# A graph layer with linear attention on one core: the work before the gathers put in another order, the gate kept turned, the gathers without a bounds operand

## The reference

```python
def _L0_gnn_ref(x, W, bias, rows, cols):
    n = x.shape[0]
    h = x @ W.T + bias
    deg = jax.ops.segment_sum(jnp.ones(rows.shape, x.dtype), rows, num_segments=n)
    norm = jax.lax.rsqrt(1.0 + deg)[:, None]
    h = norm * h
    agg = jax.ops.segment_sum(h[cols], rows, num_segments=n)
    h = agg + h
    return norm * h
...
    qkv = (x @ Wqkv).reshape(b, n, 3, h, d)
    q, k, v = (qkv[:, :, 0], qkv[:, :, 1], qkv[:, :, 2])
    k = jax.nn.softmax(k, axis=1)
    context = jnp.einsum('bnhd,bnhv->bhdv', k, v)
    out = jnp.einsum('bnhd,bhdv->bnhv', q, context).reshape(b, n, c)
    ...
    hgate = jax.nn.gelu(xn @ Wg1 + bg1, approximate=False)
    gate = jax.nn.sigmoid(hgate @ Wg2 + bg2)
    return out * gate @ Wproj + bproj
...
xn = _layernorm(x, axis=-1)
x = x + _L0_gnn_ref(xn, ..., src, dst) + _L0_mix_ref(xn[None], ...)[0]
x = x + _L0_ffn_ref(_layernorm(x, axis=-1)[None], ...)[0]
```

## Time and profile before

| | us |
|---|---|
| three runs: lowest, median, highest | 1666.53, 1668.29, 1668.53 |
| the profiled execution | 1666.09 |
| its span in the trace | 1664.4 |
| first gather issued | 473.96 |
| last gather issued | 1584.64 |
| mean granted clock of TensorE, as a share of 2.4 GHz | 0.901 |

### The profile page before, as it was taken

The page is one execution under the profiler, slowest core; times in us unless marked ns, Lnnn a source line. Parts: engine busy times, 40 slices in busy tenths (PEclk is TensorE's granted clock), DMA queues, the critical chain, the costliest instruction groups (busy, mean ns, idle before and its releaser), DMA issues.

```text
span 1664.4 us, 32504 instructions
## 1 busy us (share of the span) xinstructions
PE 1219.0 (73%) x7498; PEld 1007.9 (61%) x7499; DVE 964.7 (58%) x3571; ACT 401.8 (24%) x1361; POOL 993.5 (60%) x1055
## 2 busy tenths in 40 slices
PE   1327888869997876877877887778787877877643
PEld 1326677648875665766666666666666656666432
DVE  7799999999814542544444543444444434444347
ACT  4603656643431110111111111111111101111000
POOL 0002656640047777777777777777777777777700
PEclk9657989979998998999999998999999989999876
DMA  9100111110035556555556566655555565655624
GB/s 237 32 1 15 50 38 46 51 32 0 0 94 164 165 165 157 166 165 164 165 164 165 166 165 160 163 166 163 164 166 165 163 165 164 166 163 162 145 31 155
DMA packets 92721, 209.10 MB, mean 126 GB/s; under 512 B 29009, under 2 KB 49736, under 8 KB 92068
## 3 DMA queue, kind: packets, MB, share of 16 engines
q0 software_dynamic: 53760, 165.20, 36.4%
q1 hardware_dynamic: 24098, 25.72, 5.7%
q10 hardware_dynamic: 14834, 17.88, 3.8%
HBM read 192.31 MB, written 16.00 MB: 125 GB/s over the span
## 4 chain that ended last, share of the span: by engine, by line
POOL 30%; DVE 26%; issue 21%; PE 15%; DMA 6%; DVEq 1%; POOLq 0%; SPq 0%; ACT 0%
POOL gath L350 30%; PE bank L735 5%; DMA gath<-table,idx_stage 4%; DVE big_t L881 4%; DVE keyB L960 3%; DVE keyA L960 3%; PE bank L682 3%; PE bank L685 3%; DVE keyB L959 2%; DVE keyA L959 2%; DVE gath L879 1%; DVE kmax L952 1%; PE bank L691 1%; PE bank L578 1%; DVE big_g L1250 1%
## 5 line engine op out<-in xcount | busy, mean ns | idle before, releaser
L350 POOL DMA_INDIRECT gath<-table,idx_stage x840 | 853.6, 1016 | 370.0 <-issue 361.1
L735 PE MATMUL bank<-gath,onehot 128*125 x1680 | 353.9, 359 | 247.3 <-SPq L275 171.4
L735 PEld LDWEIGHTS bank<-gath,onehot 128*125 x1680 | 235.6, 144 | 359.4 <-issue 333.6
L1096 DVE TENSOR_SCALAR onehot<-iota_b,row_of 128x125 bf16 x840 | 170.9, 290 | 139.1 <-issue 137.6
L1107 DVE SCALAR_TENSOR_TENSOR h_res<-big_g,bank 125x256 f32<-125x256 f32 x50 | 21.1, 422 | 397.4 <-PE bank L754 397.4
L530 ACT ACTIVATE vv<-bank 128x250 f32<-128x250 f32 x50 | 19.0, 379 | 803.1 <-PE bank L775 803.1
L783 PEld LDWEIGHTS bank<-vv,w_sb 128*128 128x128 f32 x1600 | 189.6, 195 | 6.4 <-ACT vv L530 1.6
L783 PE MATMUL bank<-vv,w_sb 128*128 128x125 f32 x1600 | 189.6, 278 | 0.9 <-ACT vv L530 0.9
L793 PE MATMUL bank<-w_sb,keyB 128*125 128x256 f32 x800 | 180.9, 379 | 0.0
L793 PEld LDWEIGHTS bank<-w_sb,keyB 128*125 128x125 f32 x800 | 146.1, 188 | 19.8
L536 ACT ACTIVATE keyB<-bank,b_sb 128x125 f32<-128x125 f32 x400 | 112.9, 366 | 159.8 <-PE bank L783 149.9
(11 more groups left out here) (246 smaller groups left out, 1843.9 us busy)
## 6 DMA issues: line engine op xcount, KB each, us to landing
gath<-table,idx_stage POOLq DMA_INDIRECT x840, 3.2
table<-parts SPq DMA_DIRECT2D x50, 187.5 KB
parts<-table ACTq DMA_DIRECT2D x50, 187.5 KB
h_s<-in_x ACTq DMA_DIRECT2D x50, 125.0 KB
big_g<-in_x SPq DMA_DIRECT2D x5, 1120.0 KB
out<-big_g SPq DMA_DIRECT2D x10, 560.0 KB
w_sb<-in_L_ffn_w SPq DMA_DIRECT2D x2, 1024.0 KB
gath<-in_L_mix_Wqkv ACTq DMA_DIRECT2D x1, 768.0 KB
```

The source lines that it names most:

```text
L350: g.indirect_dma_start(out=gath[:, j, :], out_offset=None, in_=table[:, :], in_offset=bass.IndirectOffsetOnAxis(ap=idx_stage[:, j:j + 1], ...
L735: last = t.matmul(bank[0][0:P, 0:hi - lo], onehot_g[:, hot_slots, u * 128:u * 128 + P].rearrange("p a r -> p (a r)"), gath_g[:, slots, u * ...
L1096: last = nc.vector.tensor_scalar(onehot_g[:, slots, u * 128:u * 128 + P].rearrange("p a r -> p (a r)"), iota_b[:, 0:P], row_of[:, bass.ds( ...
```

## The change

1. **Before the sort.** The gate's constant and the sign step come ahead of histogram 1. Four, five and seven early sort stages (`LEADS`) stand between the histograms and behind them, ten of them before; the statistics stand behind histogram 1.
2. **Pass zero.** What needs no degree runs for all 50 windows from histogram 1 on, written out without loops: scaling, turning, storing, hidden row, keys of two windows in one product of 250 columns, gate. TensorE's last two histograms stand ahead of its windows 6 and 14. The first 16 windows of `xnT` lie in the tiles of w1 and w2 while `big_t` is in use; SP moves them and then loads w1 and w2.
3. **peek** is one instruction for two windows, 25 in all and one more at the end, and `KMAX_AT` falls from 374 to 297 quarters.
4. **One later pass** behind `kmr`: keys, values and context of window m, then the table rows of windows 2m + 2 and 2m + 3. The sorted keys are turned ahead of window 40. The copies of `xnT` into `xT` are gone, the products read `big_t`.
5. **The gate is kept turned** (128 x 250) and so is the attention's result: two transposes (L761) and ScalarE's copies (L519, L524) go from every window.
6. **The gathers** have no bounds operand.

```diff
-SORTED_BY = 19
-PEEK = 7
-LAST_PEEK = PEEK * NW
-KMAX_AT = LAST_PEEK + 24
+NB_KT = 2
+PEEK_FROM, PEEK, PEEK_LEAD = 7, 17, 12
+KMAX_AT = PEEK * (NPAIR - 1 - PEEK_FROM) + 8
+HELD = 16
+HIST_AT = (6, 14)
+KEYS_AT = 40
+LEADS = (4, 9, 16)
...
+            sp.wait_ge(s["hist"], NHIST + 1)
+            sp.wait_ge(s["xstore"], HELD)
+            for n in range(2):
+                sp.dma_start(big_t[:, n * 8:(n + 1) * 8, 0:2 * P],
+                             held[n][:, 0:8 * 2 * P].rearrange("p (w c) -> p w c", w=8)).then_inc(s["moved"], 16)
+            sp.wait_ge(s["moved"], 32)
+            sp.wait_ge(s["kT"], HELD // 2)
+            sp.dma_start(w1_sb[:, :, :], w1.rearrange("(c p) n -> p c n", p=128)).then_inc(s["wload"], 16)
+            sp.dma_start(w2_sb[:, :, :], w2.rearrange("(c p) n -> p c n", p=128)).then_inc(s["wload"], 16)
...
                     g.tensor_tensor(hgb[:, j, :], hg[:, j, :], bg1_bc[:, :], ALU.add).then_inc(s["hgb"], 1)
 
+            with g.Fori(0, NPAIR) as i:
+                for j in range(2):
+                    w = i * 2 + j
                     g.wait_ge(s["hev"], w + 3)
...
-            last_row = g.to_reg(NODES - 1)
...
-                                in_offset=bass.IndirectOffsetOnAxis(ap=idx_stage[:, j:j + 1], axis=0),
-                                bounds_check=last_row, oob_is_err=True).then_inc(s_slot[j], 16)
+                                in_offset=bass.IndirectOffsetOnAxis(ap=idx_stage[:, j:j + 1],
+                                                                    axis=0)).then_inc(s_slot[j], 16)
...
+            for m in range(NW):
+                if m + 1 < NW:
+                    stored(m + 1)
+                hidden_out(m)
+                if m:
+                    gate_turned(m - 1)
+                if m + 2 < NW:
+                    scaled(m + 2)
+                activated(m)
+                if m:
+                    gate_out(m - 1)
...
+            def h_out(m):
+                j = m % 2
+                a.wait_ge(s["main"], m + 1)
+
+                a.wait_ge(s["split"], m + 1)
+
+                a.wait_ge(s["tabfree"], m + 1)
+                a.activation(h_s[:, j, :], bank[j][0:P, 0:C], ACT.Identity, scale=norm[:, m:m + 1])
+                a.activation(parts[:, j, 0, :], bank[j][0:P, 0:C], ACT.Identity,
+                             scale=norm[:, m:m + 1]).then_inc(s["hev"], 1)
...
+            a.wait_ge(s["normd"], 1)
+            h_out(0)
...
+            h_out(1)
+            for m in range(NW):
+                exponents(m)
+                for n in (2 * m + 2, 2 * m + 3):
+                    if n < NW:
+                        h_out(n)
...
+            turn(0)
+            for m in range(NW):
+                if m in HIST_AT:
+                    histogram(2 + HIST_AT.index(m))
+                if m == HIST_AT[1]:
+                    t.matmul(bank[3][:, 0:NW], ident_b[:, :], zeros_b[:, 0:NW], start=False, stop=True,
+                             skip_group_check=True).then_inc(s["hist"], 1)
+                if m == HIST_AT[1] + 2:
+                    t.wait_ge(s["nwt"], 1)
+                    t.matmul(bank[3][:, 64:64 + NW], ones[0:P, 0:128], deg[:, :], start=True, stop=True).then_inc(s["cntp"], 1)
+                if m + 1 < NW:
+                    turn(m + 1)
+                hidden(m)
+                if m % 2:
+                    keys(m // 2)
+                if m:
+                    turn_gate(m - 1)
+                    gate(m - 1)
...
+            t.wait_ge(s["rowsh"], 1)
+            main(0)
+            main(1)
+            t.wait_ge(s["kmaxd"], NPAIR + 1)
...
+            t.wait_ge(s["kmr"], 1)
+            for m in range(NW):
+                if m == KEYS_AT:
+                    t.wait_ge(s["sortd"], 1)
+                    for b in range(COLS // 128):
+                        last = t.transpose(bank[2 + b // 4][:, (b % 4) * 128:(b % 4 + 1) * 128],
+                                           sorted_keys[:, b * 128:(b + 1) * 128], ident[:, :])
+                    last.then_inc(s["keyp"], 1)
+                keys_values(m)
+                if m:
+                    contexts(m - 1)
+                for n in (2 * m + 2, 2 * m + 3):
+                    if n < NW:
+                        main(n)
...
             def attention(m):
 
-                t.wait_ge(s["staged"], m + 1)
                 t.wait_ge(s["og"], m + 1)
-                for c in range(2):
-                    last = t.matmul(bank[1][0:P, 0:C], xT[:, 0, c, :], Wqc[:, c, :], start=c == 0, stop=c == 1)
+                for half in range(2):
+                    for c in range(2):
+                        last = t.matmul(bank[1][:, half * P:(half + 1) * P], Wqc[:, c, half * 128:(half + 1) * 128],
+                                        xnT[:, bass.ds(m, 1), c, :].rearrange("p a n -> p (a n)"), start=c == 0, stop=c == 1)
                 last.then_inc(s["op"], 1)
 
-            def turn_gated(m):
+            def project(m):
...
+            def lead(lo, hi):
+                for k, e in early[lo:hi]:
+                    local_stage(k, e, 0, EARLY, open_keys=False)
+
+            histogram(1)
+            lead(0, LEADS[0])
+            v.wait_ge(s["bna"], NW)
+            step(nc.vector.tensor_scalar(var[:, :], var[:, :], 1.0 / C, None, ALU.mult))
+            step(nc.vector.tensor_scalar(nwt[:, 0, :], var[:, :], EPS, None, ALU.add))
+            inverse_sqrt(rstd[:, :], nwt[:, 0, :], nwt[:, 1, :])
+            step(nc.vector.tensor_tensor(nmr[:, :], mean_n[:, :], rstd[:, :], ALU.mult))
+            step(nc.vector.tensor_tensor(nwt[:, 0, :], var[:, :], rstd[:, :], ALU.mult))
+            step(nc.vector.tensor_tensor(nwt[:, 0, :], nwt[:, 0, :], rstd[:, :], ALU.mult))
+            step(nc.vector.tensor_scalar(nwt[:, 0, :], nwt[:, 0, :], EPS, None, ALU.add))
+            inverse_sqrt(r2[:, :], nwt[:, 0, :], nwt[:, 1, :])
+            v.sem_inc(s["stats"], 1)
+            histogram(2)
+            for _ in range(2):
+                peek()
+            split_row(rows_h, "wmain", 16 * 9)
+            v.sem_inc(s["rowsh"], 1)
+            lead(LEADS[0], LEADS[1])
+            peek()
+            histogram(3, between=peek)
+            for _ in range(2):
+                peek()
+            lead(LEADS[1], LEADS[2])
...
-                if n < NW and stages[0] >= PEEK * (n + 1):
-                    v.wait_ge(s["kT"], n + 3)
-                    step(nc.vector.tensor_reduce(kmax2[:, :], bank[4 + 3 * (n % 2)][:, 0:2 * P].rearrange("p (h n) -> p h n", h=2),
-                                                 AX.X, ALU.max))
-                    nc.vector.tensor_tensor(kmax[:, :], kmax[:, :], kmax2[:, :], ALU.max).then_inc(s["kmaxd"], 1)
-                    v.wait_ge(s["kmaxd"], n + 3)
-                    peeks[0] += 1
+                v.wait_ge(s["kT"], n + 1)
+                nc.vector.tensor_reduce(kpart[:, n, :], bank[KT_BANK[n % NB_KT]][:, 0:4 * P].rearrange("p (h n) -> p h n", h=2),
+                                        AX.X, ALU.max).then_inc(s["kmaxd"], 1)
+                peeks[0] += 1
...
+                    if peeks[0] < NPAIR and stages[0] >= PEEK * (peeks[0] - PEEK_FROM) - PEEK_LEAD:
+                        peek()
+                        if peeks[0] == NPAIR:
+                            v.wait_ge(s["kmaxd"], NPAIR)
+                            nc.vector.tensor_reduce(kmax[:, :], kpart[:, :, :].rearrange("p i h -> p h i"), AX.X,
+                                                    ALU.max).then_inc(s["kmaxd"], 1)
...```

TensorE, around the wait for `kmr` (L682 is keys and values, L671 the turned maximum). Before, up to the loop over pairs of windows:

```order
L641 MATMUL bank<-ident,hact 64x125 [waits s_hact,s_ghT]
L646 MATMUL bank<-Wg_b,hgT 125x256 [waits s_gate,s_ghT]
L671 MATMUL bank<-ident,kmax 1x128 [waits s_gate,s_kmaxd]
L671 MATMUL bank<-ident,kmax 1x128
L675 MATMUL bank<-zeros_b,ident 128x129 x2
L682 MATMUL bank<-gath,xT 125x256 [waits s_ekv,s_stage,s_kmr]
L682 MATMUL bank<-gath,xT 125x256
L683 MATMUL bank<-rows_b,ones_b 125x256
L685 MATMUL bank<-gath,xT 125x256 x2
```

383 lines of the change are left out of this document (145 added, 238 removed).

## The result

| | before | after |
|---|---|---|
| median of the runs, us | 1667.7 | 1690.3 |
| the profiled execution | 1666.1 | 1692.7 |
| first gather issued | 473.96 | 553.21 |
| last gather issued | 1584.64 | 1611.24 |
| from there to the end of the span | 79.8 | 79.7 |

The ratio is 1.0133 (95% interval 1.0111 to 1.0155): slower by 22.6 us. The forecast was 1705, its range 1600 to 1722. But the 26.6 us between the two profiled executions are two differences, neither of which the forecast had: the first gather comes **79 us later** (it had 37), and the stretch of gathers is **52.7 us shorter** (it had 0). The tail is what it was.

A forecast was written before the change was run, and what follows sets the result against it. POOL's own pace in the 840 gathers was taken to bound two thirds of the span. The median 1668.3 plus 37 us for a later first gather, all else 0, gave 1705 us; own range 1688 to 1722, with rivals 1600 to 1722.

The forecast's parts named there:

- the front as forecast: Part before the gathers: first gather at 511 us where it was 474, a cost of 37 us.
- The gathers' price: Gathers without their bounds operand: gain taken as 0 of the 1.01 us each, the rest kept for the range.
- Rival A: Gathers: the bound was a compare per index on POOL; at 0.1 us a gather 1621 us; chance 0.38.
- Pass zero at 3.0 us a window: TensorE's windows beside the histograms: 3.0 us each, without the table row's 1.3; the sort goes on at 161 us.
- Rival C: Pass zero keeps 4.2 us a window, TensorE and ScalarE waiting in turn; sort restarts at 173, 1722 us; chance 0.05.
- Sort up to kmr: VectorE's sort of 297 quarter-stages, with transposes and reductions: 140 us, so kmr at 301 us.
- The rows: Table rows in the later pass: 7.1 us a pair beside the sort, 6.6 behind; POOL's last row kmr + 171.
- That the end of keys and values "adds nothing": Later pass: keys and values end at kmr + 227, before the 17th gather needs its slot, adding nothing.
- the sentence that the time is the first gather plus a fixed rest: Whole span: the time is the start of the first gather, plus 1110.7, plus 79.8 us.
- The turned gate and the unrolling at 0: Windows: two transposes and two ScalarE copies fewer each, and fewer register steps, gain 0 while POOL bounds.
- SP's moves at 0: SP's queue: two moves inside SBUF and the w1 and w2 loads ahead of the table stores cost nothing.
- VectorE idle from about 420 to over 500: Before the gathers: VectorE, its sort ended, stands idle from about 420 to over 500 us before copying the keys.

The follow-up runs named there:

- the two runs on the bound: Kernel before with only the gathers' bounds operand left out: 1615.5 us, ratio 0.9687; changed kernel with that operand put back: 1742.4 us, ratio 1.0445.
- the run without the bias: Changed kernel without POOL's addition of the gate's bias, ScalarE taking gelu of hg itself: 1662.3 us, ratio 0.9972.
- the ten buffers: Changed kernel with ten buffers, in the gathers' slots, for the split table rows where it had two: 1653.7 us, ratio 0.9931.
- the last one: Changed kernel with ten buffers, bias on TensorE, 30 table rows ahead of kmr, looks 15 quarters apart, sorted keys ahead of window 43: 1595.2 us, ratio 0.9579.

## Why the prediction was right in its number and wrong in two of its steps

The time lay in the range, and in the narrower one of 1688 to 1722, and the sign was the likelier one. That was luck. Of the forecast's 15 us too many, 10 are what remains of +42 and -53 in the profiled runs; the rest is how these lie beside their medians. With the bound at its true price and the front as forecast, the sum would have been 1705 - 52 = 1653 us, faster than before: the sign came out right only because the front was missed too, by 42 us.

**The gathers' price** was the term that failed most: "I take 0, the nearest row being the gather itself". It is 0.06 us of 1.01, 52 us in all (the two runs on the bound). Rival A had the right term and the point from which it decides (0.045 us a gather); that the operand costs POOL time is shown, that a compare of the indices is the reason is not. Its time of 1621 us did not come because its price was 0.1 us and its front +37: at 0.06 us that front gives 1653, and with the measured +79 about 1695. No row of before could split the 1.01; a single run did.

**Pass zero at 3.0 us a window** was the second. Up to histogram 2 the steps came as told (its end at 103.6, 104 told). Then the second peek waited 9.5 us, histogram 3 ended at 152 (136 told) and the sort went on at 193.03 (161 told). The price of POOL's addition was read from the earlier trace rows, 0.5 us, in a stretch without histograms. Without the additions a window took 2.7 us where nothing of VectorE held it, so the 3.0 was no bad price of TensorE's own; what failed was the neighbour on POOL, and the looks at the keys. Rival C said that pass zero would be slower, the sort from 173 on, but for another reason, TensorE and ScalarE in turn; the run without the bias shows nothing of that (6 us are left, beside 7.6 us of waits for VectorE).

**Sort up to kmr**, 140 us told: 333.02 - 193.03 = 140.0. The sum held, the counts of stages by size are those of the trace, and the reduction of 500 columns took 0.68 us (0.7 told).

**The rows** were told as 7.1 us a pair beside the sort and 6.6 behind it: the two pairs shown took 7.23 and 6.69. A few pairs beside the exchanges of partitions took up to 9.9 (h_res at 435.31 and, two windows on, at 445.20), so POOL's last row came kmr + 178.6 where 171 was told, the keys at kmr + 211.2 (201), the first gather 9.0 us behind them, as told. Together 10 us. That the pace is the buffers' was right (the ten buffers).

**That the end of keys and values "adds nothing"** held by some 4 us only in the changed kernel (L700 ends at 569.6, the 17th gather starts at 573.4); with the keys ahead of window 24 it failed, and with it the sentence that the time is the first gather plus a fixed rest.

**The turned gate and the unrolling at 0**: the stretch from first to last gather was 1058.0 us with and 1059.3 without them (the kernel before without its bound), and TensorE's busy time in it 844.5 and 842.7 us: the transposes went, 19.1 us in all, but the attention's products in halves took 64.1 us where they had taken 56.1, and several other groups came out 1 to 3 us longer. ScalarE's fell from 166.5 to 133.1 us, where it isn't the bound. The turned gate alone was not run.

SP's moves at 0: right, VectorE and TensorE have no wait for them. First gather told at 511: came at 553.2. VectorE idle from about 420 to over 500: it stood 85.9 us up to 545.3.

## What to carry to other kernels

Ask of each optional operand of an instruction that sits 840 times on the bounding engine what it costs; one run tells, and here it was worth more than a new schedule of the whole front (52 us, against 75 lost by the first schedule and some 20 won by the last). Before a step is moved on GpSimd, look at what VectorE does at its new place: the duration read at the old one holds only beside the same neighbour. And where a pass is moved to another time, count the moved engine's idle time at both places: from the first product after histogram 1 to the gathers TensorE was busy 345 of 471 us in the changed kernel (1690 us) and 324 of 380 in the last one (1595 us); most of the 91 us were gaps.
